# A graph layer with counting and gathering edge groups: filler matmuls removed, gathered groups placed by TensorE cycles, paired one-hot instructions, a late bias add

## The reference

```python
msg = node_feat[src] + edge_feat
neigh = segment_sum(msg, dst, num_segments=N)
rst = (1 + eps) * node_feat + neigh
h = rst @ W1 + b1                      # 128 -> 256
h = (h - mean(h, 0)) * rsqrt(var(h, 0) + 1e-5) * gamma + beta
out = relu(h) @ W2 + b2                # 256 -> 128
x = layernorm(x + out)                 # over the 128 features
```

## Time and profile before

| what | value |
|---|---|
| median of 3 runs (lowest, highest) | 280.51 us (279.13, 280.87) |
| the profiled execution's own time | 281.48 us |
| its span, first to last instruction | 279.7 us |
| mean granted TensorE clock, share of full speed | 0.964 |
| TensorE matmuls busy | 244.9 us (88%) |
| VectorE busy | 208.4 us (75%) |
| GpSimd busy | 181.2 us (65%) |
| ScalarE busy | 131.7 us (47%) |
| bytes moved by DMA | 38.39 MB |

### The profile page before, as it was taken

The page is one execution under the profiler, slowest core; times in us unless marked ns, Lnnn a source line. Parts: engine busy times, 40 slices in busy tenths (PEclk is TensorE's granted clock), DMA queues, the critical chain, the costliest instruction groups (busy, mean ns, idle before and its releaser), DMA issues.

```text
span 279.7 us, 7102 instructions
## 1 busy us (share of the span) xinstructions
PE 244.9 (88%) x2211; PEld 200.6 (72%) x2211; DVE 208.4 (75%) x916; ACT 131.7 (47%) x236; POOL 181.2 (65%) x117
## 2 busy tenths in 40 slices
PE   1567989999998889988899999999999859999970
PEld 1456768899987677766788888777878648844870
DVE  3888997788998778778489887876867861178990
ACT  0327864455555535545255544444443302086494
POOL 2078888888888888888888888888888920000000
PEclk9999999999999999999599999999999968999995
DMA  5955766687888777788488888776665200000033
GB/s 165 285 172 108 147 145 137 156 191 197 189 195 185 178 164 171 181 179 183 96 172 192 174 195 171 167 179 145 150 126 105 53 2 0 2 0 1 2 114 116
DMA packets 49535, 38.39 MB, mean 137 GB/s; under 512 B 5083, under 2 KB 48523, under 8 KB 49497
## 3 DMA queue, kind: packets, MB, share of 16 engines
q1 hardware_dynamic: 32829, 30.62, 38.2%
q0 software_dynamic: 14976, 6.82, 20.4%
q10 hardware_dynamic: 1692, 0.48, 0.9%
HBM read 36.31 MB, written 1.60 MB: 136 GB/s over the span
## 4 chain that ended last, share of the span: by engine, by line
PE 46%; DMA 16%; issue 14%; POOL 9%; DVE 7%; ACT 4%; SPq 2%; DVEq 0%; ACTq 0%; POOLq 0%
PE ps L641 18%; PE ps L649 12%; DMA egat<-in_x_dram,srci 9%; POOL egat L402 9%; DMA egat<-in_edge_attr_dram 7%; PE ps L679 5%; PE ps L673 4%; PE ps L595 4%; ACT big L527 3%; PE ps L665 2%; SPq L321 1%; DVE big L1033 1%; DVE big L1035 1%; PE ps L670 1%; DVE hit_l L904 1%
## 5 line engine op out<-in xcount | busy, mean ns | idle before, releaser
L402 POOL DMA_INDIRECT egat<-in_x_dram,srci x104 | 172.2, 1656 | 44.0 <-issue 29.2
L488 ACT ACTIVATE big<-ps 128x500 f32 x156 | 95.1, 610 | 119.8 <-PE ps L679 91.6
L641 PE MATMUL ps<-big,xp 128*128 128x114 f16 (+8 forms) x675 | 116.9, 280 | 0.2 <-issue 0.2
L649 PEld LDWEIGHTS ps<-hit_c,ebuf 128*128 128x128 f32 x624 | 101.8, 194 | 16.6 <-DVE aggT L983 6.1
L649 PE MATMUL ps<-hit_c,ebuf 128*128 128x20 f32 x624 | 95.1, 230 | 9.1 <-DVE aggT L983 5.0
L641 PEld LDWEIGHTS ps<-big,xp 128*128 128x128 bf16 x675 | 63.0, 110 | 14.6 <-issue 1.1
L983 DVE TENSOR_TENSOR aggT<-aggT,ps 128x20 f32 x208 | 35.8, 172 | 49.8 <-PE ps L649 39.7
L910 DVE TENSOR_TENSOR hit_k<-iota_k,key 128x400 f16<-128x400 f16 x156 | 56.1, 359 | 0.0
L904 DVE TENSOR_TENSOR hit_l<-iota_k,lo 128x256 f16<-128x256 f16 x156 | 52.1, 334 | 1.7 <-issue 1.6
L679 PE MATMUL ps<-hit_k,hit_l 128*128 128x400 f16 x156 | 52.3, 335 | 0.0
L908 DVE TENSOR_TENSOR hit_k<-iota_k,key 128x300 f16<-128x300 f16 x156 | 48.2, 309 | 0.0
(11 more groups left out here) (101 smaller groups left out, 165.5 us busy)
## 6 DMA issues: line engine op xcount, KB each, us to landing
ebuf<-in_edge_attr_dram SPq DMA_DIRECT2D x78, 256.0 KB
egat<-in_edge_attr_dram SPq DMA_DIRECT2D x51, 128.0 KB
egat<-in_x_dram,srci POOLq DMA_INDIRECT x104
out_dram<-big SPq DMA_DIRECT2D x6, 256.0 KB
w_sb<-in_L_gnn_W_dram ACTq DMA_DIRECT2D x2, 128.0 KB, 6.8
rows<-in_dst_dram SPq DMA_DIRECT2D x1, 192.0 KB
rows<-in_src_dram ACTq DMA_DIRECT2D x1, 192.0 KB
egat<-in_edge_attr_dram SPq DMA_DIRECT2D x1, 66.0 KB
```

The source lines that it names most:

```text
L402: return nc.gpsimd.indirect_dma_start(to, None, x[:, :], bass.IndirectOffsetOnAxis(ap=ix, axis=0), compute_op=op)
L488: nc.scalar.activation(cnt[:, :, bass.ds(lows[m % LOADS], WIN)], ps[:, m % BANKS_C, 0:KEYS].rearrange("p (t n) -> p t n", n=WIN), ACT.Copy ...
L641: last = nc.tensor.matmul(ps[:, ACC + f % 2, 0:SIZES[f]], xp[:, t, n, :], cnt[:, t, STARTS[f]:STARTS[f] + SIZES[f]], start=(u == 0), stop= ...
L649: last = nc.tensor.matmul(ps[:, SUMS + w % BANKS_S, 0:WIN], rows_v[:, j * D:(j + 1) * D], hits_v, start=(j == 0), stop=(j == ROWS - 1))
```

## The change

It sets KEEP = 0 (no L665). GC becomes 158 and NG 50, with 22 groups in the seventh block, now 332 columns wide (before 20 and 302). `in_window` gives way to `arrange()`, which lays the windows out in cycles of TensorE: 670 for a gathered and 1430 for a counted window, the block's columns + 6 for each unit, 1660 for the transposes and at least 3000 for each of the first 14 windows. It makes a window gathered when the running sum passes 16000 + n x step, the step such that 50 of them fill the total. Worked through, the gathered windows are 6, 9, 12, 15, 19, 24, 29, 34, ... (every fifth), later every fourth, and 192, 195, 197, 200, 203, 206, 207 at the end; the total is 461420 cycles.

`hits_k` runs for even groups and makes two groups with three instructions of 512, 600 and 800 elements, AHEAD = 4, in a ring of 8. The operand for the carry one-hot becomes fp16. `xp` and ScalarE's copies go: the first two parts are read as the upper halves of the float32 words of `xN` and `xr`, every second bf16 element. GpSimd's b2 add also waits until the last block is multiplied. At the end, the activation of half 1 moves to ScalarE for the last two of 7 blocks, the 7 pieces become 8 (five of 4 tiles, then 2, 2 and 1), and VectorE normalises the seventh.

```diff
-GROUPS_C = 156
-BLOCKS_C = (10, 12, 17, 25, 31, 31, 20, 8, 2)
+GROUPS_C = 158
+BLOCKS_C = (10, 12, 17, 25, 31, 31, 22, 8, 2)
-RING_K = 6
-AHEAD = 3
+RING_K = 8
+AHEAD = 4
-KEEP = 24
+KEEP = 0
+SUM = 670
+COUNT = 760
+HITS = 3000
+TURN = 1660
+GAP = 6
+GATHER_FIRST = 16000
+ACT_FROM = 5
-    def in_window(w):
-        return (w + 1) * NG // G > w * NG // G
+    def arrange():
...
+                if total:
+                    gathered = n < NG - 1 and (m == GC or now >= GATHER_FIRST + n * step) or w == G - 1
...
+                own = SUM if gathered else SUM + COUNT + KEPT * (KEEP_FROM <= m < KEEP)
+                now += max(own + TURN * (X_RATE * w < NT), HITS * (w < SPREAD * NB)) + (u1 - u0) * (SIZES[f] + GAP)
...
                 pool.wait_ge(x_rest_made, NB)
-                pool.wait_ge(x_first_made, NB)
+                pool.wait_ge(block_multiplied, F)
...
-                        nc.scalar.activation(xp[:, t0:t1, 0, :], upper(xN[:, t0:t1, :]), ACT.Copy).then_inc(x_first_made, 1)
-                        act.wait_ge(x_rest_made, b + 1)
-                        nc.scalar.activation(xp[:, t0:t1, 1, :], upper(xr[:, b % 2, 0:t1 - t0, :]),
-                                             ACT.Copy).then_inc(x_middle_made, 1)
...
-                        last = nc.tensor.matmul(ps[:, ACC + f % 2, 0:SIZES[f]], xp[:, t, n, :],
+                        part_v = x3[:, t, :] if n == 2 else upper((xN, xr)[n][:, t:t + 1, :])[:, 0, :]
+                        last = nc.tensor.matmul(ps[:, ACC + f % 2, 0:SIZES[f]], part_v,
...
-                    nc.vector.tensor_tensor(hit_l[:, r, :, :].rearrange("p j (n two) -> p j n two", two=2),
-                                            pairs(iota_k[:, 0:P]).unsqueeze(1).to_broadcast([P, ROWS, P // 2, 2]),
-                                            lo[:, 2 * m:2 * m + 2, :].unsqueeze(2).to_broadcast([P, ROWS, P // 2, 2]),
+                    nc.vector.tensor_tensor(hit_l[:, r:r + 2, :, :].rearrange("p g j (n two) -> p (g j) n two", two=2),
+                                            pairs(iota_k[:, 0:P]).unsqueeze(1).to_broadcast([P, 2 * ROWS, P // 2, 2]),
+                                            lo[:, 2 * m:2 * m + 4, :].unsqueeze(2).to_broadcast([P, 2 * ROWS, P // 2, 2]),
...
-                        if m + AHEAD < GC:
+                        if m % 2 == 0 and m + AHEAD < GC:
...
+    ROW_PIECES = [(t, t + 4) for t in range(0, NT - 5, 4)] + [(NT - 5, NT - 3), (NT - 3, NT - 1), (NT - 1, NT)]
```

More of the change, by code:

```diff
@@ L82, in gnn_layer, with spans, share @@
     KEYS = NT * WIN
-    def in_window(w):
-        return (w + 1) * NG // G > w * NG // G
-    C_AT = [w for w in range(G) if not in_window(w)]
-    G_AT = [w for w in range(G) if in_window(w)]
+    UNITS = NT * PARTS
+    def spans(c_at):
+        return [c_at[g - 1] + SETTLE for g in ENDS[:-1]] + [G]
+    def share(ready, w):
+        for f in range(F - 1):
+            if ready[f] <= w < ready[f + 1]:
+                n, i = ready[f + 1] - ready[f], w - ready[f]
+                return f, UNITS * i // n, UNITS * (i + 1) // n
+        return 0, 0, 0
+    def arrange():
+        order = [(w + 1) * NG // G > w * NG // G for w in range(G)]
+        total = 0
+        for _ in range(ROUNDS):
+            ready = spans([w for w in range(G) if not order[w]])
+            step = (total - GATHER_FIRST) / (NG - 1)
+            old, now, m, n, order = order, 0, 0, 0, []
+            for w in range(G):
+                if total:
+                    gathered = n < NG - 1 and (m == GC or now >= GATHER_FIRST + n * step) or w == G - 1
+                else:
+                    gathered = old[w]
+                f, u0, u1 = share(ready, w)
+                own = SUM if gathered else SUM + COUNT + KEPT * (KEEP_FROM <= m < KEEP)
+                now += max(own + TURN * (X_RATE * w < NT), HITS * (w < SPREAD * NB)) + (u1 - u0) * (SIZES[f] + GAP)
+                order.append(gathered)
+                m, n = m + (not gathered), n + gathered
+            total = now
+        return order
+    IN_WINDOW = arrange()
+    C_AT = [w for w in range(G) if not IN_WINDOW[w]]
+    G_AT = [w for w in range(G) if IN_WINDOW[w]]
     C_OF = {w: m for m, w in enumerate(C_AT)}
     G_OF = {w: n for n, w in enumerate(G_AT)}
-    READY = [C_AT[g - 1] + SETTLE for g in ENDS[:-1]] + [G]
-    UNITS = NT * PARTS
+    READY = spans(C_AT)
     def units(w):
[L95 to L99, removed]
+        return share(READY, w)
+    ROW_PIECES = [(t, t + 4) for t in range(0, NT - 5, 4)] + [(NT - 5, NT - 3), (NT - 3, NT - 1), (NT - 1, NT)]
     EARLY = STARTS[-1] // BANK
@@ L145, in gnn_layer @@
         lsd, lrs, lnb = (part(NT) for _ in range(3))
+        bag = part(HH * 2).rearrange("p (h s) -> p h s", s=2)
+        sd, rsd, scl, ms, sft = (part(HH) for _ in range(5))
         at[0] = 0
@@ L370, in _ @@
                         chunk(C_OF[w] // CHUNK + CHUNKS)
-            for b in range(NB):
-                t0, t1 = pieces(b)
+            for t0, t1 in ROW_PIECES[:6]:
                 sp.wait_ge(rows_normalised, t1)
[L375 to L379, removed]
+                sp.dma_start(out_v[:, t0:t1, :], oN[:, t0:t1, :]).then_inc(rows_written, 16)
+            t0, t1 = ROW_PIECES[6]
+            sp.wait_ge(late_rows_normalised, t1 - t0)
+            sp.dma_start(out_v[:, t0:t1, :], oN[:, t0:t1, :]).then_inc(rows_written, 16)
+            sp.wait_ge(rows_normalised, NT - 2)
+            sp.dma_start(out[(NT - 1) * P:N, :], oN[0:NL, NT - 1, :]).then_inc(rows_written, 16)
+            sp.wait_ge(rows_written, 16 * len(ROW_PIECES))
         @block.gpsimd
@@ L740, in _ @@
                     for h in range(HH):
-                        last = nc.tensor.matmul(ps[0:r, (b + 4) % 8, k:k + D], hT[:, h, t * P:t * P + r], w2_sb[:, h, :],
+                        last = nc.tensor.matmul(ps[0:r, (a + 4) % 8, k:k + D], hT[:, h, t * P:t * P + r], w2_sb[:, h, :],
                                                 start=False, stop=(h == HH - 1), skip_group_check=True)
@@ L951, in _ @@
                 hits_c(0)
-                hits_k(1)
                 hits_n(0)
@@ L1027, in _ @@
             dve.wait_ge(scale_steps, 4)
-            for b in range(NB):
+            for b in range(ACT_FROM):
                 r = rl[:, b % 2, 0:width(b)]
@@ new lines, in stats, with moments @@
+            def stats(a):
+                t0, t1 = ROW_PIECES[a]
+                r = rows_of(t1 - 1)
+                dve.wait_ge(rows_made, a + 1)
+                for t in range(t0, t1):
+                    k = (t - t0) * D
+                    nc.vector.bn_stats(lst[0:r, t, :], ps[0:r, (a + 4) % 8, k:k + D]).then_inc(row_stats_made, 1)
+            def moments(a):
+                t0, t1 = ROW_PIECES[a]
+                r = rows_of(t1 - 1)
+                for t in range(t0, t1):
+                    dve.wait_ge(row_stats_made, t + 1)
+                    nc.vector.bn_aggr(lag[0:r, t, :], lst[0:r, t, :]).then_inc(row_moments_made, 1)
@@ new lines, in _ @@
+            for a in range(len(ROW_PIECES)):
+                stats(a)
+                if a > 0:
+                    shifts(a - 1)
+                moments(a)
+            t0, t1 = ROW_PIECES[6]
+            dve.wait_ge(row_shifts_made, 7)
+            for t in range(t0, t1):
+                k = (t - t0) * D
+                nc.vector.tensor_scalar(oN[:, t, :], ps[:, 2, k:k + D], lrs[:, t:t + 1], lnb[:, t:t + 1],
+                                        ALU.mult, ALU.add).then_inc(late_rows_normalised, 1)
```

140 lines of the change are left out of this document (65 added, 75 removed).

## The result

| | before | after |
|---|---|---|
| median, us (lowest to highest, executions) | 280.69 (279.13 to 280.93, 4) | 271.62 (271.23 to 275.44, 4) |
| ratio, 95% interval | | 0.968 [0.964, 0.972] |
| profiled execution: own time, span | 281.48, 279.7 | 271.86, 270.1 |
| first hidden matmul to the end of the span | 36.4 | 35.4 |

Faster by 3.2%, 9 us, where 24.5 were forecast; 271.6 lies 7.6 us above the range (252 to 264).

What follows compares the result with a forecast made beforehand. GpSimd's gathers were taken to pace the long middle, TensorE the wide blocks after window 168. Hidden matmuls at 218.6 + (279.7 - 243.3) - 0.9 gave a 254.1 us span; with 1.8 more, 256 us, range 252 to 264.

Steps and rivals of the forecast that it cites:

- What bounds the kernel: GpSimd's gathers, 3.87 us each, pace the long middle; TensorE paces after window 168, when units are wide.
- both engines would arrive together: End of the windows: GpSimd's last gather ready at 213.6, TensorE alone done at 214.0; 215.0 taken for both.
- the gain forecast for the even spacing: Middle windows: gathers asked for each 3.79 us against 3.87 delivered, removing TensorE's idle waits; no separate size given.
- the rival "Clock": Windows 9 to 13: without fillers TensorE's clock may fall, 3 us a fall, giving 259 or 262 us; chance 0.18.
- Windows 0 to 15: VectorE paces these; paired one-hots save 0.6 us, so window 16 starts at 39.2 instead of 39.84.
- TensorE from window 16 on: TensorE's work: 172.9 us plus 1.9 for narrow blocks, alone ending window 207 at 214.0.
- Removing the fillers takes out 8.1 us: TensorE from window 16 on: 24 filler pairs of 0.34 us each no longer take its time.
- The b2 add moved: GpSimd's add runs beside the hidden matmuls, covered by 3 us; the old stall and slow clock behind it cost about 7.5.
- it does not hold the statistics: Hidden stage: the add costs VectorE's statistics nothing; the rival that it holds VectorE cost 4.1 us, chance 0.08.
- Weights with a step of two elements: Weight loads in 50 of a block's 75 units: no cost taken; rival of slower loads, 272 to 291 us, chance 0.03.
- The end: Last normalising after the W2 matmuls: handing two activation blocks to ScalarE saves 0.9 us, bounds 0 and 1.4.
- Sum: Whole kernel: hidden matmuls at 218.6, span 254.1 us, execution 256 us with 1.8 added.

Runs made afterwards that it cites:

- b_keep0: The kernel before with its 24 groups of fillers removed and nothing else: 281.26 us, ratio 0.997.
- KEEP = 12: The changed kernel with two filler matmuls in each of the first 12 counted groups only: 260.9 us, ratio 0.933.
- the early matmuls: The changed kernel with fillers in the first 12 counted groups and 11 more before window 0: three executions at 260.5 to 261.2 us, two at 274.9 and 275.3.

## Why the prediction was wrong, step by step

**What bounds the kernel**: right for before (b_keep0 above: 12.6 us of delay vanish in the middle), and GpSimd kept its pace: the last gather was to be ready at 213.6, and with KEEP = 12 it starts at 209.81, ready some 3.9 us later, with a mean of 1.657 + 0.30 us in denser traffic (1.656 + 0.30 in the earlier trace rows). That both engines would arrive together was not so. Window 207 starts at 217.9, TensorE waits for no gather, and with the old rule of every fourth window it waits for none either. TensorE alone paces, and the gain forecast for the even spacing is not shown.

**The step that failed**: the rival "Clock", and with it the sentence that the fillers of windows 0 to 15 are worth nothing "as long as the clock holds". The mechanism was named, its chance put at 0.18 and its price at "each fall costs 3 us". The price came from the two falls that the earlier trace rows shows late, beside 376- and 302-column units, from which the level came back after 6.8 us each. A fall before the 114-column block, without fillers behind it, lasted 41 us in after. It cost 14 us in two executions of one kernel, and 12.3 in the profiled pair of after and KEEP = 12 (hidden matmuls at 234.71 and 222.41). The forecast had them at 218.6: of the 16.1 us missed, these 12.3 are the level, and 3.8 are the terms below. The chance was wrong too: without fillers both profiled executions have the loss, and all 8 take 271.2 us or more. The argument against, that the gaps there are short, judged single waits; the level fell behind one of 0.62 and, with fillers, outlived one of 1.45.
The Trainium skill, "TensorE: Matmul & The Clock Gate", section "Part 1", has the lower level as the default that sustained activity lifts, and calls the ramp under 1% of a typical span. The first half was the right warning; on the second this case's runs differ: 12 of 271 us, 5%, with a matmul in flight without a gap for the last 25 of the 41 us.

**Windows 0 to 15**: 39.2 forecast for window 16; 42.2 in after, at half speed, 40.65 with KEEP = 12. The one-hots shrank as computed, but waits of 1.45 and 1.33 us for adds, which the budgets left out (the text said so), took it back. Without pairs no wait there for an add is longer than 0.54.

**TensorE from window 16 on**: from there to the hidden matmuls 179.4 us forecast; 181.8 with KEEP = 12: 1.0 for three short waits for adds, the rest rows a little longer than the sum. In after it is 192.5. Without pairs it is 179.8. From window 16 to 34 alone after takes 28.2 us (42.17 to 70.33) and KEEP = 12 15.2 (with one gathered window more and one counted less): 13.0, more than the 12.3 of the whole. "Removing the fillers takes out 8.1 us" was the right size for TensorE's time (12 of them 3.7 measured), the wrong account of what they did.

**The b2 add moved**: 7.5 forecast, 7.3 in the profiled pair, 5.3 by the medians; the pair is an execution of before above its median (281.48) and the fastest of the other (274.18). That it does not hold the statistics was right.
The Trainium skill, "SBUF — State Buffer", section "Who interferes with whom", says the same of an instruction with one SBUF input, and now both halves stand in rows: 7.95 us for the one-hot with two, 0.69 for the statistics with one.

**Weights with a step of two elements**: no cost, as taken: the three operands' matmuls average 288, 289 and 288 ns, their loads 113 to 116 ns, which include 41 us at half speed; with KEEP = 12 the loads take 107 to 109 ns, against 110 before. Units of 110 columns start 0.047 to 0.05 us apart.

**The end**: 0.9 forecast, 1.0 measured (36.4 to 35.4).

**Sum**: 260.9 with KEEP = 12 against 256 leaves 4.9: 1.45 for window 16, 2.4 to the hidden matmuls, and 1.3 because the profiled execution was the fastest of four (259.6; 254.1 + 3.85 + 1.8 = 259.75, less 0.1 in the end). Its mean clock is 0.993, that of the others 0.982 to 0.988, so they may have lost the level for a few us.

**The best version** is the change with fillers in the first 12 counted groups: 260.9 us, 7% below before and 4% below the change. Without pairs it is 259.3, but of 13 executions with 12 fillers and the narrow first block (with pairs 4, without 4, with the early matmuls 5) three took 274 to 275, with mean clocks of 0.921 to 0.931; the one of them with a trace had lost the level. With 17 groups (261.9) none of four did; that is few executions, and the safer choice rests on them. What makes the level fall in one execution and not in the next stays open.

## What to carry to other kernels

Before removing a filler or any work that keeps TensorE busy, ask what the matmuls behind it look like: here, beside 114-column units, a lost level stayed lost through the whole stage, and its price was that stage's matmul time nearly once more (13.0 on 15.2 us), not the length of one recovery seen elsewhere. A kernel paced by another engine can hide this price, as before did; the change that takes the waits for that engine away makes it due, so test the filler's removal within the new version and not in the old one. Read the level from the duration of one repeated matmul, since the clock row draws a level that has not changed yet as full.

## What the runs showed of the hardware

- TensorE stayed at 1.2 GHz while it always had a matmul in flight: 45 to 69 us in after, 29 to 72 us before without fillers, both with 20-, 25-, 300-, 400- and 114-column matmuls, and 180-column units in the last 7 or 8 us. It returned 5.3 to 7.6 us after the first 180-column unit (in after 62.86, back at 69.5), 4.9 and 3.4 us after the first 294-column unit, and 5.7 us after 400-column fillers joined the 114-column units.
- A loss elsewhere lasted 6.8 us (twice in before), 3.4 us (before with the late b2 add) or 10.2 us (the same with KEEP = 12, among 256-column units).
- The granted-clock row starts at full whatever the level is: 300-column matmuls last 0.43 to 0.46 us until 20 or 21 us in before, in after and with KEEP = 12, under a row of 9.
- The same kernel has two times, 261 and 275 us, and the slow one that has a trace is at half speed from 34 to 71 us.
- A GpSimd add of 7 us beside VectorE statistics disturbs neither (6.98 us after 7.55 in before, 0.69 after 0.695); the same add beside a two-operand one-hot holds it for 7.95 us.
